# Letting each gather of embedding rows wait for the landing of the last gather but one, in a fused recommendation tower

## The reference

```python
x = layer_norm(dense_t @ Wd.T, gd, bd)                  # 512 x 128
y = layer_norm(einsum('bnd,ed->bne', sparse_t, Ws))     # 26 rows a sample, 64 -> 128
y = layer_norm(einsum('bne,pn->bep', y, Wsi))           # mix 26 features to 32
T = concatenate([x, y])                                 # 33 vectors of 128
Z = einsum('bnd,bmd->bnm', T, T)                        # their products in pairs
out = layer_norm(Zflat @ Wl.T) * mask                   # 528 pairs -> 512, 384 used
h = relu(concat([out, dense_t]) @ W_top1 + b_top1)      # then 512 -> 256 -> 1
```

## Time and profile before

| | |
|---|---|
| Median of 3 runs | 195.09 us (193.76 to 196.07) |
| Profiled execution | 194.37 us, span of its instructions 192.5 us |
| Granted TensorE clock | 0.965 in the mean |
| PE busy | 147.8 us (77%) |
| POOL busy | 101.2 us (53%), of it 100.3 us in 104 gathers |
| DVE, ACT busy | 99.6 us, 89.7 us |

### The profile page before, as it was taken

The page is one execution under the profiler, slowest core; times in us unless marked ns, Lnnn a source line. Parts: engine busy times, 40 slices in busy tenths (PEclk is TensorE's granted clock), DMA queues, the critical chain, the costliest instruction groups (busy, mean ns, idle before and its releaser), DMA issues.

```text
span 192.5 us, 4176 instructions
## 1 busy us (share of the span) xinstructions
PE 147.8 (77%) x1644; PEld 96.4 (50%) x1644; DVE 99.6 (52%) x192; ACT 89.7 (47%) x225; POOL 101.2 (53%) x113
## 2 busy tenths in 40 slices
PE   0495596949595964698869858788695789988996
PEld 0333544434354442455447637455565566446674
DVE  2481937684908475567074838270848266541001
ACT  3613154554433549355555436336645446641251
POOL 4777374767637287657674775776757730000000
PEclk9999579999998897899999999999999999999999
DMA  5713131417201011632110154211111650025000
GB/s 147 269 29 76 34 116 20 129 24 258 70 14 27 10 27 27 146 70 33 24 27 14 30 134 79 38 32 20 21 24 20 150 78 4 3 67 105 6 3 0
DMA packets 20260, 11.58 MB, mean 60 GB/s; under 512 B 12945, under 2 KB 17681, under 8 KB 20242
## 3 DMA queue, kind: packets, MB, share of 16 engines
q1 hardware_dynamic: 16226, 7.83, 15.4%
q0 software_dynamic: 3328, 3.41, 9.4%
q10 hardware_dynamic: 688, 0.08, 0.3%
HBM read 9.15 MB, written 2.16 MB: 59 GB/s over the span
## 4 chain that ended last, share of the span: by engine, by line
PE 43%; POOL 20%; DMA 13%; DVE 9%; issue 8%; ACT 5%; POOLq 1%; SPq 0%; ACTq 0%
POOL e_rows L372 20%; DMA e_rows<-table_dram,rows_sb 8%; PE mix_ps L439 7%; PE proj_ps L473 5%; PE o_ps L487 5%; PE quad_ps L450 4%; PE dots_ps L464 3%; PE o_ps L421 3%; PE o_turn_ps L402 3%; PE turn_ps L431 2%; DVE e_unit L909 2%; DVE e_prod L881 2%; DVE var_n L884 2%; PE dots_ps L395 2%; DMA z_dram<-z_mine 2%
## 5 line engine op out<-in xcount | busy, mean ns | idle before, releaser
L372 POOL DMA_INDIRECT e_rows<-table_dram,rows_sb x104 | 100.3, 965 | 54.2 <-issue 28.0
L439 PE MATMUL mix_ps<-mixw_sb,e_unit 128*128 128x192 f32 (+4 forms) x128 | 23.4, 329 | 17.9 <-DVE e_unit L909 17.9
L439 PEld LDWEIGHTS mix_ps<-mixw_sb,e_unit 128*128 128x128 f32 x128 | 20.5, 202 | 26.3 <-DVE e_unit L909 26.0
L881 DVE TENSOR_TENSOR e_prod<-quad_ps,e_rows 128x384 f32<-128x384 f32 (+1 forms) x16 | 9.5, 591 | 45.6 <-PE quad_ps L450 45.6
L473 PE MATMUL proj_ps<-f_sb,proj_w 128*128 128x512 f32 x60 | 31.7, 611 | 0.1
L872 DVE TENSOR_REDUCE var_p<-y_sq 128x16 f32<-128x512 f32 x32 | 20.5, 677 | 1.6 <-ACT y_sq L664 1.6
L679 ACT COPY f_sb<-mix_ps 64x512 f32<-64x512 f32 x32 | 18.5, 578 | 5.4 <-PE mix_ps L439 5.0
L487 PE MATMUL o_ps<-wl_sb,z_pairs 128*128 128x512 f32 (+1 forms) x40 | 18.8, 600 | 1.7 <-DMA z_pairs<-s_dram 1.2
L664 ACT ACTIVATE y_sq<-proj_ps 128x512 f32<-128x512 f32 x30 | 17.6, 587 | 4.8 <-PE proj_ps L473 4.6
L896 DVE TENSOR_TENSOR feats<-proj_ps,rstd_p 128x512 f32<-128x512 f32 x30 | 19.3, 686 | 0.6
L450 PEld LDWEIGHTS quad_ps<-gram,e_cols 128*128 128x128 f32 x104 | 13.6, 195 | 11.1 <-ACT e_cols L672 11.0
(11 more groups left out here) (142 smaller groups left out, 173.3 us busy)
## 6 DMA issues: line engine op xcount, KB each, us to landing
z_dram<-z_mine SPq DMA_DIRECT2D x4, 512.0 KB, 3.3
e_rows<-table_dram,rows_sb POOLq DMA_INDIRECT x104, 2.5
w_sb<-w_dram SPq DMA_DIRECT2D x2, 512.0 KB, 6.2
wl_sb<-wl_dram SPq DMA_DIRECT2D x2, 512.0 KB, 3.4
w_sb<-w_dram SPq DMA_DIRECT2D x1, 768.0 KB, 4.8
dense_sb<-dense_t_dram SPq DMA_DIRECT2D x1, 512.0 KB, 4.5
wl_sb<-wl_dram SPq DMA_DIRECT2D x1, 256.0 KB, 2.8
z_pairs<-z_dram SPq DMA_DIRECT2D x4, 64.0 KB, 2.1
```

The source lines that it names most:

```text
L372: pool.indirect_dma_start(out=e_rows[:, chunk, t, D * ab:D * (ab + 1)], out_offset=None, in_=table, in_offset=bass.IndirectOffsetOnAxis(ap ...
L439: mm = pe.matmul(mix_ps[:, PR * at:PR * (at + number)], e_unit[:, t, :], mixw_sb[:, t, lo:lo + number, :].rearrange("k b p -> k (b p)"), s ...
```

## The change

Each slot gets two semaphores, one for each half `ab`, and every gather adds to that of its half. The gathers of the halves alternate, so the gather before the last one is the previous one of the same half. Before each gather POOL waits until that one has landed: at the first tile of a slot, until the last tile of the slot before it has, in the same half. The first two gathers of all wait for none. after_round and its waits are gone. All who wait for a slot's rows now wait for both semaphores (rows_landed).

```diff
--- before.py
+++ after.py
@@ -230,7 +230,8 @@
         ids_in, small_in, mixw_in, dense_in = sem("ids_in"), sem("small_in"), sem("mixw_in"), sem("dense_in")
         w1_in, wl_in, w2_in, out_done = sem("w1_in"), sem("wl_in"), sem("w2_in"), sem("out_done")
         pairs_in, w1_dense_in = sem("pairs_in"), sem("w1_dense_in")
-        gathered = [[sem(f"gathered{chunk}_{q}") for q in range(QUARTERS)] for chunk in range(CHUNKS)]
+        gathered = [[[sem(f"gathered{chunk}_{q}_{ab}") for ab in range(2)] for q in range(QUARTERS)]
+                    for chunk in range(CHUNKS)]
         rows_ready = sem("rows_ready")
         consts = sem("consts")
         prep_dve, prep_pe, prep_act = sem("prep_dve"), sem("prep_pe"), sem("prep_act")
@@ -263,6 +264,10 @@
         def place(s):
             return s // QUARTERS, s % QUARTERS
 
+        def rows_landed(eng, chunk, q):
+            for ab in range(2):
+                eng.wait_ge(gathered[chunk][q][ab], 16 * tiles_of(q)[1])
+
         def wait(eng, semaphore, count):
 
             if not isinstance(count, int) or count > 0:
@@ -307,10 +312,10 @@
             sp.dma_start(pairs_sb[:], pairs).then_inc(pairs_in, 16)
 
             for q in range(3):
-                sp.wait_ge(gathered[0][q], 32 * tiles_of(q)[1])
+                rows_landed(sp, 0, q)
                 begin, end = q * KZ // 3, (q + 1) * KZ // 3
                 sp.dma_start(wl_sb[:, begin:end, :], wl[:, begin:end, :]).then_inc(wl_in, 16)
-            sp.wait_ge(gathered[0][3], 32 * tiles_of(3)[1])
+            rows_landed(sp, 0, 3)
             sp.dma_start(w1_sb[:, 0:KU, :], w1[:, 0:KU, :]).then_inc(w1_in, 16)
             sp.dma_start(w2_sb[:], w2).then_inc(w2_in, 16)
 
@@ -355,24 +360,26 @@
             pool.memset(feats[:, :, :, 0], 1.0).then_inc(consts, 1)
             pool.wait_ge(rows_ready, 1)
 
-            def after_round(i):
-                if i >= 2:
-                    pool.wait_ge(dotted, i - 1)
-                elif i >= 0:
-                    pool.wait_ge(mixed, i + 1)
-                    pool.wait_ge(gathered[0][i + 1], 32 * tiles_of(i + 1)[1])
+            def second_last_landed(s, t, ab):
+
+                chunk, q = place(s)
+                if t > tiles_of(q)[0]:
+                    pool.wait_ge(gathered[chunk][q][ab], 16 * (t - tiles_of(q)[0]))
+                elif s > 0:
+                    chunk, q = place(s - 1)
+                    pool.wait_ge(gathered[chunk][q][ab], 16 * tiles_of(q)[1])
 
             for chunk in range(CHUNKS):
                 for q in range(QUARTERS):
-                    after_round(chunk * QUARTERS + q - 2)
                     t0, nt = tiles_of(q)
                     for t in range(t0, t0 + nt):
                         for ab in range(2):
+                            second_last_landed(chunk * QUARTERS + q, t, ab)
                             col = (chunk * TILES + t) * 2 + ab
                             pool.indirect_dma_start(
                                 out=e_rows[:, chunk, t, D * ab:D * (ab + 1)], out_offset=None, in_=table,
                                 in_offset=bass.IndirectOffsetOnAxis(ap=rows_sb[:, col:col + 1], axis=0),
-                            ).then_inc(gathered[chunk][q], 16)
+                            ).then_inc(gathered[chunk][q][ab], 16)
 
         @block.tensor
         def _(pe):
@@ -425,7 +432,7 @@
             def turn(s):
                 chunk, q = place(s)
                 t0, nt = tiles_of(q)
-                pe.wait_ge(gathered[chunk][q], 32 * nt)
+                rows_landed(pe, chunk, q)
                 wait(pe, cols_ready, s)
                 for t in range(nt):
                     mm = pe.transpose(turn_ps[:, P * t:P * (t + 1)], e_rows[:, chunk, t0 + t, :], eye_sb)
@@ -877,7 +884,7 @@
                 t0, nt = tiles_of(q)
                 dve.wait_ge(quad_done, s + 1)
                 wait(dve, std_ready, s)
-                dve.wait_ge(gathered[chunk][q], 32 * nt)
+                rows_landed(dve, chunk, q)
                 dve.tensor_tensor(e_prod[:, 0:2 * nt, :].rearrange("p a d -> p (a d)"), quad_ps[:, 0:P * nt],
                                   e_rows[:, chunk, t0:t0 + nt, :].rearrange("p t d -> p (t d)"), ALU.mult).then_inc(prod_done, 1)
                 dve.wait_ge(prod_done, s + 1)
```

## The result

The changed kernel is slower: its runs stand to those of before as 1.050, with a 95% interval of 1.034 to 1.065. Four executions took 203.0, 204.1, 208.8 and 211.8 us; the ratio is made of the first two, since executions over 1.5% above the fastest are left out, and the median of all four is 206.45; the kernel before took 192.9 to 196.1 beside them, median 194.4. The profiled execution took 203.0 around a span of 201.2 us; before it was 194.4 around 192.5. I had forecast slower, 198.5 us and at most 202.6. The direction and the mechanism were right, the size was not: in the profiled executions 8.7 us came where I had 3.9.

What follows compares the result with a forecast made beforehand. Gather landings on POOL were taken to set the last turn: 145.9 us quiet plus 15.6 for late landings gives 161.5 instead of 157.6, +3.9 us. That made 198.3 for the profiled execution, forecast 198.5, range 193.6 to 202.6.

Steps and rivals of the forecast that it cites:

- The pace: POOL's gathers: landing 2.45 us plus 0.27 start makes a pair 2.72 us instead of 2.50, pitch 1.36.
- What the old waits gave: POOL's removed waits for mix and pair products: 24.3 us of idleness, eaten by quiet waits (11 us) and late ones (15.6).
- rival 1: The landing wait on POOL is free, pitch stays near 1.25; 8.1 us earlier, 186 to 187 us; chance 0.12 including halfway.
- PE's own chain needs 131.5 us: PE from slot 0's turn to slot 15's: 142.3 us less 10.8 of waiting for gathers.
- the late landings: Each late gather landing now delays POOL's whole row: 17.3 us listed, 15.6 counted, last landing at 161.5.
- SP's transfers: Gathers landing late beside SP's transfers: opening 2.75 us, weights 3.0, three z moves 1.35 each.
- what I took off for absorption: Delays in one of the two alternating gather chains are partly taken up before reaching the other: 1.7 us off for 17 events.
- the quiet row: POOL's 104 gathers without late landings, a pair each 2.72 us: the last lands at 145.9 us.
- Instruction packets and slow descriptors: Gathers delayed by instruction-queue packets, five of some ten counted, 5.5 us; seven gathers with longer descriptors, 2.0 together.
- rival 3: More late landings on POOL, all ten packets meeting a gather: 20 us and more, last turn at 166, 203 us; chance 0.13.
- The tail, the turn of slot 0: The stretch behind PE's last turn should stay 34.9 us; PE's first turn comes near 18 instead of 15.35.
- The rule against the pace: The skill's DMA fit gives gather landings of 2.08 us; the wait would never bind in quiet stretches, about 186 us.

Runs made afterwards that it cites:

- the two other kernels whose gathers ran ahead: Changed kernel with each gather waiting for the last but two: 0.985; kernel before without POOL's gather waits, ScalarE issuing two of nine z reads: 0.972.
- the separate row: Changed kernel's 104 gathers and waits without its computation; last gather starts: alone 139.5 us, plus SP's transfers 153.2, plus TensorE's many instructions 163.5, or few instead.
- the 10.3 of the table: Gathers beside SP's transfers, with TensorE's many instructions added: last gather starts at 163.5 us against 153.2 without them, 10.3 more.

## Why the prediction was right in direction and wrong in size

- **The pace.** Right. Landing 2.45, start 0.26 later, 2.71 us a pair in quiet stretches; the double wait at consumers cost nothing that could be measured.
- **What the old waits gave.** They were eaten by the pace, as forecast. The kernel without them and without the new ones shows that they alone were worth 1.5%, not the 8 us of rival 1. Its price rested on "PE's own chain needs 131.5 us". That step was wrong: hardly held by gathers the chain took 152.7 - 15.1 = 137.6 us, and 137.9 and 138.1 in the two other kernels whose gathers ran ahead. A wait that I subtracted was covering another one just behind it. Turn to turn, less the waits for gathers, three stretches of the kernel without waits are longer than before: slot 6 to 7 by 2.9 us (ACT's copy behind the scaling of `wl_sb`), 3 to 4 by 2.2 (a lower granted clock in the products with `pick`), 11 to 12 by 1.6 (z's return, 2.0); the other twelve come to -0.6. Taking z's wait away didn't shorten this chain. The tail grew by 3.4 us, 1.85 of it z, the rest at a granted clock of 0.58 from 157.9 to 162.0; whether the wait brought the lower clock isn't shown. For the changed kernel this changes nothing: at 19.4 + 137.6 PE would have come to the last turn near 157, and the gathers came at 166.4.
- **The failed step: the late landings.** "The late landings cost 15.6 us" was the term that was mis-sized: the last landing was forecast at 161.5 and came at 166.4, so they cost 20.5 over the 145.9 of the quiet row; the chain's 20 late ones sum to 20.6. Two of its parts were off: SP's transfers by 4.0, and what I took off for absorption by 1.7.
  - Transfers: I had 9.8 us (opening 2.75, weights 3.0, z three times 1.35); the late landings beside SP's loads and z writes come to 13.8 in the changed kernel's chain, and the separate row shows 13.7. 2.4 of this was left out altogether. These are the three loads of wl, with 3.4 and 3.5 us at 28.0 and 37.1; in the kernel before, the second fell where POOL stood waiting for mix products, so that no gather in 22:32 was late, and the third hides in the stretch 32:41 behind its 3.7. The opening gave 6.0 us and not 5.2, the weights 5.8 and not 5.4, and the third z move, for which I had no row and took the first, 4.4.
  - Instruction packets and slow descriptors: I had 7.5, and this term was not too small. The chain's other late landings come to 6.8, of it 5.8 in nine with a packet in flight. Counted from my quiet row of 143.5 the separate rows say the same, 164.0 - 143.5 - 13.7 = 6.8; the 10.3 of the table starts from the 139.5 that the quiet row really took. The make-up was off: I counted five of ten packets as hitting a gather, at 1.1 each; all ten did, one of them beside the third z move, and the nine cost 0.65 each.
  - I took 1.7 us off for delays that the other chain absorbs. The 20.6 us arrived at the last landing in full: the gap of 0.22 in a pair absorbs next to nothing of a delay of 1 to 3 us.
- **The range.** What came is rival 3, to which I gave 0.13: all ten packets met a gather, late landings summed to 20, the last turn came at 166.5. Its price of 203 us lies just beyond my 202.6. Besides, the changed kernel's own runs spread from 203.0 to 211.8 where those of before lay within 3.1 us. That a row in which every late landing counts spreads with them is my explanation; no trace of a longer run was kept to show it.
- **The tail, the turn of slot 0.** 34.7 against 34.9; the turn came at 19.4 against "near 18", for the opening's sake.
- **The rule against the pace** (the Trainium skill, DMA: Bandwidth & Descriptors, section Anatomy of one DMA, 2.0 us and the bytes at 436 GB/s, an estimate of 2.08 here). The trace doesn't agree: alone, with nothing beside them, gathers of this size landed 2.3 to 2.5 us after their start, and POOL stood waiting for a landing before 98 of the gathers.

## What to carry to other kernels

A wait for the landing of an earlier DMA is free only if the landing and the start behind it fit into the pitches between; here 2.45 + 0.26 against 2 x 1.25 made it bind nearly always, and with three pitches, 3.75, only twelve gathers were held and the row ended before PE's last turn. Such a wait turns every late landing anywhere into lost time for the whole queue, so count what else moves beside the row, also where the queue now rests and the trace shows nothing late. And before you subtract an engine's waits to find its own time, look for the next wait that stands just behind them: here 2.8 us of waiting for gathers hid 3.2 us of waiting for ScalarE.

## What the runs showed of the hardware

- POOL started a gather 0.26 us after its release (once 0.28), whether by a matrix product or by a landing, all along the chain.
- Fetching TensorE's instructions takes part in the traffic that delays gathers: 13 packets against 1 beside a row of 104 went with 6.2 us, and each of the 13 was in flight in a pair of gathers of over 2.9 us instead of 2.6 to 2.7.
- Ordinary landings, those up to 2.6 us, differed by chip: 2.36 to 2.38 us in the mean of all gathers in the four kernels profiled on one chip, 2.42 to 2.44 in the six on another. Over fifty pairs in a chain that is some 3 us.
- The changed kernel's granted TensorE clock was 0.941 in the mean, that of before 0.965, with PE waiting more; nothing of the 8.7 us comes from it, since PE isn't in the chain before the last turn, and behind it the clock was 1.00 in both.
